# VectorE: the split of the sums T of h in front of layer 1's second block sum

## The reference

```
h = gelu(einsum('bni,ih->bnh', x, W1) + b1, approximate=False)      # 512 -> 2048
shared_x = einsum('bnh,ho->bno', h, W2) + b2                        # 2048 -> 384
expert_x = einsum('bnh,bhp->bnp', h, We[indices]) + be[indices]     # 2048 -> 128
out = x + concatenate([shared_x, expert_x], axis=-1)
```

## Time and profile before

| | |
|---|---|
| median of 3 runs | 1255.66 us (1255.28 to 1255.77) |
| profiled execution | 1254.18 us, its span 1252.4 us |
| TensorE busy | 1240.2 us, 99% of the span |
| weight loads | 925.0 us, 74% |
| VectorE busy | 940.6 us, 75% |
| ScalarE busy | 743.1 us, 59% |
| granted clock of TensorE | full in all 40 slices, mean 1.000 |
| DMA | 64.45 MB, mean 51 GB/s |

### The profile page before, as it was taken

How to read it: one execution, slowest core, us unless ns; L and a number is a source line. 1 busy time by engine, 2 the same in 40 slices (tenths; PEclk the granted TensorE clock), 3 DMA queues, 4 the chain that set the end, 5 groups by cost and what they waited for, 6 DMA issues and landing times.

```text
span 1252.4 us, 23996 instructions
## 1 busy us (share of the span) xinstructions
PE 1240.2 (99%) x9473; PEld 925.0 (74%) x9473; DVE 940.6 (75%) x1201; ACT 743.1 (59%) x944; POOL 0.2 (0%) x4
## 2 busy tenths in 40 slices
PE   9999999999999999999999999999999999999998
PEld 5446667777777777778777778778777777777775
DVE  7966658777688787787777687786787877777765
ACT  3744556656566565666656665665666656666562
POOL 0000000000000000000000000000000000000000
PEclk9999999999999999999999999999999999999999
DMA  7211322002020020201102020020200202011000
GB/s 302 68 68 59 110 68 76 27 1 102 1 94 7 0 100 0 101 0 37 63 0 101 0 67 34 0 101 0 101 0 17 84 0 101 0 52 48 1 35 34
DMA packets 25378, 64.45 MB, mean 51 GB/s; under 512 B 5120, under 2 KB 5120, under 8 KB 22016
## 3 DMA queue, kind: packets, MB, share of 16 engines
q1 hardware_dynamic: 25344, 63.99, 14.7%
HBM read 47.20 MB, written 16.78 MB: 51 GB/s over the span
## 4 chain that ended last, share of the span: by engine, by line
PE 95%; DVE 4%; ACT 1%; issue 0%; ACTq 0%
PE banks L1089 15%; PE banks L1090 15%; PE banks L1091 15%; PE out_ps L1091 9%; PE out_ps L1090 9%; PE out_ps L1089 9%; PE q_ps L1089 8%; PE q_ps L1090 8%; PE q_ps L1091 8%; DVE w_lo L668 1%; DVE w_max L654 1%; PE out_ps L1277 1%; DVE h_ring L668 1%; DVE x_lo L668 0%; DVE x_max L654 0%
## 5 line engine op out<-in xcount | busy, mean ns | idle before, releaser
L1089 PE MATMUL banks<-x_hi,w_hi 128*128 128x256 f16 (+1 forms) x1724 | 474.6, 275 | 3.9 <-ACT u L513 2.6
L1091 PE MATMUL banks<-x_hi,w_lo 128*128 128x256 f16 (+1 forms) x1724 | 474.6, 275 | 0.0
L1090 PE MATMUL banks<-x_lo,w_hi 128*128 128x256 f16 (+1 forms) x1724 | 474.6, 275 | 0.0
L668 DVE SCALAR_TENSOR_TENSOR h_ring<-u,scale,h_ring 128x2048 f16<-128x2048 f32 x120 | 281.2, 2343 | 6.9 <-ACT h_ring L438 4.8
L505 ACT ACTIVATE kept<-banks 128x512 f32<-128x512 f32 x180 | 106.3, 591 | 176.5 <-PE banks L1091 176.5
L1089 PEld LDWEIGHTS banks<-x_hi,w_hi 128*128 128x128 f16 x1724 | 168.6, 98 | 50.7 <-ACT u L513 3.1
L1090 PEld LDWEIGHTS banks<-x_lo,w_hi 128*128 128x128 f16 x1724 | 168.6, 98 | 45.1
L1091 PEld LDWEIGHTS banks<-x_hi,w_lo 128*128 128x128 f16 x1724 | 168.7, 98 | 24.2
L446 ACT ACTIVATE h_ring<-u,scale 128x2048 f16<-128x2048 f32 x56 | 112.1, 2002 | 96.7 <-DVE u L838 96.7
L870 DVE TENSOR_TENSOR u<-banks,kept 128x512 f32<-128x512 f32 x60 | 41.5, 692 | 167.4 <-PE banks L1091 153.4
L535 ACT ACTIVATE u<-u,b_sb,undo 128x512 f32<-128x512 f32 x120 | 91.2, 807 | 122.8 <-DVE u L883 122.8
(11 more groups left out here) (130 smaller groups left out, 1660.0 us busy)
## 6 DMA issues: line engine op xcount, KB each, us to landing
x_raw<-x_dram SPq DMA_DIRECT2D x64, 256.0 KB, 3.5
e_raw<-we_dram SPq DMA_DIRECT2D x16, 1024.0 KB, 4.7
out_dram<-x_raw SPq DMA_DIRECT2D x64, 256.0 KB, 2.2
h_ring<-w_dram SPq DMA_DIRECT2D x6, 1024.0 KB, 8.5
t_sum<-w2p_dram SPq DMA_DIRECT2D x2, 1024.0 KB, 4.8
w_sums<-w_dram SPq DMA_DIRECT2D x2, 768.0 KB, 15.3
x_raw<-w_dram SPq DMA_DIRECT2D x1, 1024.0 KB, 11.9
t_sum<-w_dram SPq DMA_DIRECT2D x1, 1024.0 KB, 13.9
```

Of the source, the lines that this page charges most:

```text
L668: return nc.vector.scalar_tensor_tensor(to, of, s, hi, ALU.mult, ALU.subtract)
L1089: nc.tensor.matmul(ps, hi, v_hi, start=start, stop=False, skip_group_check=True)
L1090: nc.tensor.matmul(ps, hi, v_lo, start=False, stop=False, skip_group_check=True)
L1091: return nc.tensor.matmul(ps, lo, v_hi, start=False, stop=stop, skip_group_check=True)
```

## The change

In VectorE's `batch` the call of `ht_split` moves from directly behind `c22` to directly in front of it, in all four steps.

```
                 if w2_s:
                     add_w2_s(0)
+                ht_split(b - 1, 3, 1 - par)
                 c22(b, 0)
-                ht_split(b - 1, 3, 1 - par)
...
                 if w2_s:
                     add_w2_s(1)
+                ht_split(b, 0, par)
                 c22(b, 1)
-                ht_split(b, 0, par)
...
                 if sums:
                     add_s(3)
+                ht_split(b, 1, par)
                 c22(b, 2)
-                ht_split(b, 1, par)
...
                 if loads is not None:
                     add_t(b + 1, 1 - par)
+                ht_split(b, 2, par)
                 c22(b, 3)
-                ht_split(b, 2, par)
```

## The result

The changed kernel takes 1257.49 us (median of 20 runs, 1256.49 to 1259.06) against 1255.37 us (20 runs, 1253.68 to 1256.22): a ratio of 1.0021 with a 95% interval of 1.0014 to 1.0028. It is slower by about 0.2%, inside the forecast range. The profiled execution took 1257.29 us, its span 1255.5 us, which is 3.1 us more than that of before. So the medians say 2.1 us and the two traces 3.1 us; the forecast said 2.2. Which of them is the price of the change the experiments had to settle; it is the figure of the traces.

What follows compares the result with a forecast made beforehand. TensorE was taken as the bound; 1.1 us from step 0 of batches 3 to 15 plus 1.1 us from batch 2 made 2.2 us, added to 1255.66 for 1257.8 us. The 8-in-10 range was 1256.5 to 1260.6 us.

Steps and rivals of the forecast that it cites:

- TensorE is the bound, and the change can only open holes: Whole kernel: TensorE has a matmul in flight 1240.2 of 1252.4 us; the change opens holes there or leaves it alone.
- c22 moves by 2.26 us: VectorE, swapped pairs: c22 starts one split of T later, 2.26 us after where the split now begins.
- Steps 1 to 3 pay nothing: Batches 3 to 15: c22 still signals before P3's load is due, spare 0.09, 0.18 and 0.12 us, no loss.
- Batch 2 pays 1.26 less 0.17 us: Batch 2: step 1 loses 1.26 us at P3, step 2 regains 0.17 us at a hold now there; net 1.1 us.
- A late load is paid only as far as the matmul is late: TensorE at P3: loss counts from the matmul's due time, plus 0.01 us; a late load alone is not paid in full.
- Step 0 pays 0.07 and 0.10 us: Step 0 of batches 3 to 15: P3 held by c22, 0.07 us in even and 0.10 in odd batches, 1.1 us.
- The sum: Whole run: 1.1 us from steps 0 plus 1.1 us from batch 2, 2.2 us slower, 1257.8 us.
- (a): P3's first weight load in step 0, and batch 2: late load paid in full, 5.0 us, 1260.7 us; chance 0.09.
- its milder form: Only the load itself stands bare before its matmul, 0.10 us at 14 places: 3.6 us, 1259.3 us; chance 0.09.
- (b): Step 0: the cover just holds, only batch 2 pays, 1.1 us, 1256.8 us; chance 0.15.
- (c): Batch 2 pays nothing either and the early T helps: 0.17 us gained, 1255.5 us; chance 0.02.
- (d): Steady steps: c22's lateness returns through ScalarE to the next step's c11, each losing more, above 1258.2 us; chance 0.05.

Runs made afterwards that it cites:

- the delays: Changed kernel with an extra VectorE reduce of eight different lengths in front of c22: steps lost 0.00 to 0.78 us.
- the waits: Changed kernel, P3 of step 0 waiting for c22 alone: 1257.34 us; delayed kernel with one wait in step 0, two in others: signal 0.05 against 0.11 us.

## Why the prediction was right, and where it was not

- *TensorE is the bound, and the change can only open holes.* Right. VectorE's work is the same, and the loss is the sum of fourteen holes less one that closed.
- *c22 moves by 2.26 us.* Right: 15.65 to 15.68 us after P1 in step 0.
- *Steps 1 to 3 pay nothing.* Right in all 39. Their c22 ends at 15.92 us after P1 at the latest; the delays show that c22 could have come as late as 16.25 with one wait.
- *Batch 2 pays 1.26 less 0.17 us.* Right: 1.24 less 0.18.
- *A late load is paid only as far as the matmul is late.* Right, and measured with one wait: free up to 0.2 us of lateness, 0.27 us lost at a c22 that ends at 16.55.
- *Step 0 pays 0.07 and 0.10 us.* Here a term was mis-sized. The prediction took 0.05 us for the signal from the earlier trace rows and 0.01 us from load to matmul from the earlier trace rows, and the matmul that waits has one wait in both. P3 of step 0 has two, and the wait for c22 is an instruction of its own there. The terms are 0.12 and 0.03 us, the losses 0.15 and 0.18 us, the sum 2.1 us in place of 1.1. Where a loss is a small difference of two large numbers, 0.08 us doubled it.
- *The sum.* 3.2 us in place of 2.2. That the median came out at 1257.49 us, 0.3 us from the forecast of 1257.8, is in part luck: the runs' scatter at the start hid 1 us, as much as the mis-sized term had left out. The forecast also carried the median of three runs over, all three of which lay in the upper group. By the price that the experiments show, the change is on the slower side of 0.2%, which the prediction had given 0.35.
- *Rivals.* (a) and its milder form fall by the table of delays. The milder form is what the Trainium skill's load time ("TensorE: Matmul & The Clock Gate", section "LDWEIGHTS (loading the stationary operand)", columns / 1.2) gives if a late load stands bare; the section states the duration alone, and the bare load is the prediction's own step. No row here shows it: matmuls stand 0.01 to 0.03 us behind the start of a late load. Its total of 3.6 us is nevertheless nearer to the 3.2 us measured than the forecast's 2.2, so the total could not have decided between them; the delays and the waits did. (b), the cover in step 0 just holds, was wrong by 0.15 us. (c) fell with the 1.24 us of batch 2. (d) found nothing: no steady step 1 to 3 changed its length.

## What to carry to other kernels

An operation that a busy engine needs soon must not stand behind one that is needed a step later, even if both are on an engine with a quarter of its time free: what counts is not the idle share but the distance from the end of each operation to its customer, step by step, and the tightest step decides. When that distance comes out within 0.1 us of zero, look at how many waits the customer has and for semaphore instructions of their own in its queue, and measure the response with a few graded delays in one kernel instead of trusting a signal time from another place. And where runs of one kernel scatter by more than the change is worth, find the cause in the traces first: here one hole in the start hid a third of the effect and was worth more than the change itself.

## What the runs showed of the hardware

- A matmul with two waits starts its weight load 0.11 to 0.12 us after the end of the VectorE instruction that satisfies the last of them; with one wait it is 0.05 to 0.06. Between c22 and the load there then stands a semaphore instruction of 0.05 us in TensorE's queue, fifteen in the changed kernel for P3, none with one wait, 45 with the second wait in steps 1 to 3. From the load to the matmul it is 0.03 and 0.01 us. Such a hole is put down to "issue" with two waits and to the releasing instruction with one, so that a row like the 13 holes of "issue" above can be a wait for another engine.
- With one wait, a weight load could come 0.2 us late, up to 0.01 us ahead of its matmul's due time, without any loss (16.31 against 16.32, step unchanged to 0.01 us). With two waits a load at 16.31 cost 0.02 us, and one at 16.21 nothing.
- A hole of 2.6 us in TensorE's row was followed by a granted clock of 1.2 GHz for some 3 us in four of the eight traced executions that had it; in the other four, and in the two without the hole, it stayed at 2.4 GHz.
